# One hybrid block, sixteen-head attention: the first unit's score rows inside the preparation, and row statistics taken tile by tile for the next layer

## The reference, cut to what matters

```python
x = x + A(_layernorm(x))      # gated slot attention
x = x + FFN(_layernorm(x))    # 16-head causal attention, then a mixture of 4 experts, with norms of its own
x = x + C(_layernorm(x))      # 16 heads of 16, not causal
x = x + FFN(_layernorm(x))

def _layernorm(x, axis=-1, eps=1e-05):
    m = jnp.mean(x, axis=axis, keepdims=True)
    v = jnp.var(x, axis=axis, keepdims=True)
    return (x - m) / jnp.sqrt(v + eps)

def C(x, q_w, k_w, v_w, q_b, k_b, v_b, out_w, out_b):   # cut
    q, k = apply_rope(heads(x @ q_w.T + q_b)), apply_rope(heads(x @ k_w.T + k_b))
    attn = jnp.einsum('bhqd,bhkd->bhqk', q, k) * scaling
    out = jnp.einsum('bhqk,bhkd->bhqd', softmax(attn), heads(x @ v_w.T + v_b))
    return merge(out) @ out_w.T + out_b
```

## Time and profile before

| | |
|---|---|
| median of 3 runs | 2630.3 us |
| lowest, highest | 2629.23, 2631.29 us |
| the profiled execution | 2630.27 us |
| its span in the trace | 2628.5 us |
| TensorE busy | 2331.3 us (89%) |
| VectorE, ScalarE, POOL busy | 1678.3, 1192.8, 1100.5 us |
| mean granted TensorE clock | 0.963 |

### The profile page before, as it was taken

The page is one execution under the profiler, slowest core; times in us unless marked ns, Lnnn a source line. Parts: engine busy times, 40 slices in busy tenths (PEclk is TensorE's granted clock), DMA queues, the critical chain, the costliest instruction groups (busy, mean ns, idle before and its releaser), DMA issues. The chain is left out here.

```text
span 2628.5 us, 49074 instructions
## 1 busy us (share of the span) xinstructions
PE 2331.3 (89%) x18400; PEld 1614.6 (61%) x18400; DVE 1678.3 (64%) x3286; ACT 1192.8 (45%) x2937; POOL 1100.5 (42%) x1264
## 2 busy tenths in 40 slices
PE   5888888888888889888858999999889989999999
PEld 3467754777547775477745666677533356666685
DVE  3857777577776777667726777752366557777613
ACT  3655465554554546545424555532115535555411
POOL 0367632676326763277634544430030025444300
PEclk9999999999999999999978999999889989999999
DMA  2100000000010000000004000000100030000000
GB/s 46 49 6 2 2 17 32 6 2 2 17 33 5 3 2 17 17 2 2 2 1 120 19 19 19 7 1 1 49 1 1 1 114 19 19 19 13 1 1 17
DMA packets 57625, 46.30 MB, mean 18 GB/s; under 512 B 11560, under 2 KB 50864, under 8 KB 57008
## 3 DMA queue, kind: packets, MB, share of 16 engines
q1 hardware_dynamic: 57392, 43.16, 5.6%
HBM read 42.10 MB, written 1.05 MB: 16 GB/s over the span
## 5 line engine op out<-in xcount | busy, mean ns | idle before, releaser
L1153 DVE SCALAR_TENSOR_TENSOR work<-four,taps,work 128x511 f32<-128x511 f32 (+2 forms) x384 | 284.7, 748 | 127.1 <-ACT work L849 117.5
L1761 POOL TENSOR_TENSOR rot<-q_plain,ropes 128x512 f32<-128x512 f32 x64 | 81.0, 1266 | 574.7 <-ACT q_plain L1792 574.7
L599 PE MATMUL four<-xT,wring 128*128 128x512 f32 x512 | 252.8, 621 | 6.6 <-DMA wring<-in_Wk_dram 4.8
L906 ACT ACTIVATE work<-four 128x512 f32<-128x512 f32 x216 | 129.0, 597 | 269.4 <-PE four L678 243.4
L729 PE MATMUL four<-work 128*128 128x128 f32 x1536 | 217.0, 286 | 0.0
L1805 ACT ACTIVATE pr<-four,nmaxf 128x512 f32<-128x512 f32 (+3 forms) x256 | 133.8, 525 | 171.4 <-DVE nmaxf L1643 171.4
L1643 DVE TENSOR_REDUCE nmaxf<-four 128x1 f32<-128x512 f32 (+3 forms) x256 | 125.7, 491 | 125.6 <-PE four L1486 120.8
L729 PEld LDWEIGHTS four<-work 128*128 128x128 f32 x1536 | 193.4, 196 | 3.9
L1484 PE MATMUL four<-rot,rot 128*128 128x512 f32 (+3 forms) x512 | 179.5, 446 | 5.5 <-DVE rot L1635 3.8
L1088 POOL TENSOR_TENSOR work<-work 128x256 f32<-128x256 f32 x184 | 145.6, 791 | 78.0 <-DVE work L1217 57.4
L1095 POOL TENSOR_TENSOR work<-work 128x256 f32<-128x256 f32 x184 | 141.7, 770 | 84.2 <-PE bank L763 74.6
(11 more groups left out here) (266 smaller groups left out, 5430.9 us busy)
## 6 DMA issues: line engine op xcount, KB each, us to landing
wqkv<-in_f_wq_dram SPq DMA_DIRECT2D x32, 128.0 KB, 2.3
wqkv<-in_f_wk_dram SPq DMA_DIRECT2D x32, 128.0 KB, 2.4
wqkv<-in_f_wv_dram SPq DMA_DIRECT2D x32, 128.0 KB, 2.4
wo<-in_f_wo_dram SPq DMA_DIRECT2D x2, 2048.0 KB, 11.7
we<-in_f_we_dram SPq DMA_DIRECT2D x4, 1024.0 KB
wring<-in_Wk_dram SPq DMA_DIRECT2D x4, 512.0 KB, 3.8
wring<-in_Ww_dram SPq DMA_DIRECT2D x4, 512.0 KB
wring<-in_Wv_dram SPq DMA_DIRECT2D x4, 512.0 KB, 3.9
```

The source lines that it names most:

```text
L599: last = nc.tensor.matmul(unit_bank(i)[:], wring[n % 2][:, c, h * P:(h + 1) * P], k.xT[:, c, b * T:(b + 1) * T], start=(c == 0), stop=(c = ...
L906: nc.scalar.activation(turned_keys(s, l), b3(key_bank), ACT.Copy).then_inc(key_kept, 1)
L1153: ins = nc.vector.scalar_tensor_tensor(out=cbuf[i % 4][:, n:], in0=unit_bank(i)[:, 0:T - n], scalar=taps[:, {"q": 0, "k": 1}.get(kind, 2), ...
```

## The change

It has two parts.

The first moves the row statistics. A new function `measure` takes the statistics and the aggregate of one tile, each after a wait. A, B (not D) and C call it directly after their last add to a tile, and the next layer's norm only waits for the eight. The first norm of all, before A, is as it was.

The second moves the first unit's four row groups: after the turns of parts 4, 7, 10 and 13 on TensorE, and their maxima after the rotations of parts 5, 8, 11 and 14 on VectorE. Since the groups need the banks 0 to 3, projections go to banks 4 and 5 and turns to 6 and 7. VectorE waits for POOL's zeroed tiles before the first part and not before the values.

```diff
+def measure(k, dve, stage, t):
+    nc, signal = k.nc, k.measured[stage]
+    nc.vector.bn_stats(k.stats[:, t, :], k.x[:, t, :]).then_inc(signal, 1)
+    dve.wait_ge(signal, 2 * t + 1)
+    nc.vector.bn_aggr(k.mean_var[:, t, :], k.stats[:, t, :]).then_inc(signal, 1)
...
-            for t in range(NT):
-                last = nc.vector.bn_stats(k.stats[:, t, :], src[:, t, :])
-            then(last)
-            for t in range(NT):
-                last = nc.vector.bn_aggr(k.mean_var[:, t, :], k.stats[:, t, :])
-            then(last)
+            if measured is None:
...
+            else:
+                dve.wait_ge(k.measured[measured], 2 * NT)
...
                             if t >= 2:
                                 add(g, t - 2)
-                        add(g, NT - 2)
-                        add(g, NT - 1)
+                                dve.wait_ge(x_added, (g - 1) * NT + t)
+                                measure(k, dve, 0, t - 2)
+                        for t in (NT - 2, NT - 1):
+                            add(g, t)
+                            dve.wait_ge(x_added, (g - 1) * NT + t + 2)
+                            measure(k, dve, 0, t)
...
-                for t in range(NT):
-                    last = nc.vector.bn_stats(k.stats[:, t, :], k.x[:, t, :])
-                last.then_inc(x_stats, 1)
-                dve.wait_ge(x_stats, 1)
-                for t in range(NT):
-                    last = nc.vector.bn_aggr(k.mean_var[:, t, :], k.stats[:, t, :])
-                last.then_inc(x_stats, 1)
-                dve.wait_ge(x_stats, 2)
+                dve.wait_ge(k.measured[2 * rep], 2 * NT)
...
+                        if n >= E * NT and rows is None:
+                            dve.wait_ge(y_used, n + 1)
+                            measure(k, dve, 1, t)
...
+FIRST_ROWS = {4 + 3 * r: r for r in range(CH)}
...
-                        last = nc.tensor.matmul(k.bank[i % 2][:], wqk[m][:, c, j * P:(j + 1) * P], k.xT[:, c, b * T:(b + 1) * T],
+                        last = nc.tensor.matmul(part_bank(i)[:], wqk[m][:, c, j * P:(j + 1) * P], k.xT[:, c, b * T:(b + 1) * T],
...
-                    nc.tensor.matmul(k.bank[2 + i % 2][:], turn_m[:], flat[i % 3][:], start=True, stop=True).then_inc(c_turned, 1)
+                    nc.tensor.matmul(part_turn_bank(i)[:], turn_m[:], flat[i % 3][:], start=True, stop=True).then_inc(c_turned, 1)
+                    if i in FIRST_ROWS:
+                        pe.wait_ge(c_roped, 2)
+                        score_rows(0, FIRST_ROWS[i])
...
                     for r in range(CH):
-                        if n < NC_UNITS:
+                        if 0 < n < NC_UNITS:
                             score_rows(n, r)
...
                     nc.vector.tensor_tensor(qk[m][:, j, b * T:(b + 1) * T], cs[n % 2][:], sn[n % 2][:], ALU.add).then_inc(c_roped, 1)
+                    if n - 1 in FIRST_ROWS:
+                        maximum(0, FIRST_ROWS[n - 1])
...
                     nc.vector.tensor_tensor(k.x[:, t], k.x[:, t], k.bank[t % 4][:, 0:D], ALU.add).then_inc(added, 1)
+                    dve.wait_ge(added, t + 1)
+                    measure(k, dve, 2, t)
```

## The result

| | before | after |
|---|---|---|
| median | 2630.98 us (7 runs) | 2619.26 us (7 runs, 2616.99 to 2624.64) |
| ratio | | 0.9960, 95% interval 0.9949 to 0.9970 |
| the profiled execution | 2630.27 us | 2616.99 us |
| its span | 2628.5 us | 2615.2 us |

The changed kernel is faster by 0.4%, 11.7 us by the medians and 13.3 by the two profiled executions; 13.7 was forecast. The profiled execution of after is the fastest of its seven.

A forecast was written before the change was run, and what follows sets the result against it. The attention start was taken as a ping-pong of TensorE and VectorE, the preparation as a TensorE stream with room on VectorE. Terms -1.75 - 1.74 + 2.1 - 12.3 = -13.7 from 2630.27 gave 2616.6 us, range 2612 to 2622.

The forecast's parts named there:

- first seam: Slot attention to expert block: statistics after each add bring the norm's root 1.75 us earlier, and all of it arrives.
- third seam: Attention to expert block: statistics after each add bring the norm's root 1.74 us earlier.
- second seam, tail: Expert block to attention: statistics make VectorE the pace of the last eight scaled adds, ending 2.1 us later.
- second seam, transfers: Attention's first projection awaits the last of ten transfers, which move with the block's start; nothing won back, 0.
- four groups: Four row groups added to TensorE's gapless preparation stream, 0.97 us each, 3.9 us in all.
- fourth maximum: On VectorE between the rotations of parts 14 and 15, on the path for 2.3 us; the first three cost nothing.
- clock falls in the pause: TensorE's pause before the third value tile grows to 3.5 us, the clock falls, 2.0 us lost.
- row stage gone: The first unit's row groups after the values vanish, shift transposes follow the last value tile at once: -17.07 us.
- first unit at the full clock: TensorE reaches the shift from a dense value stream at full level, so the first unit gains 3.4 us.
- rival of a broken stream: Preparation: a row group takes 2.09 us because its 32-row pieces must wait; 2621.1 us in all, chance 0.08.
- holds: Rival: the clock holds over the pause before the third value tile; 2614.6 us in all, chance 0.14.
- two rivals with a low first unit or slow units: Clock low from values into first unit, 2623.5 us, chance 0.09; units at the 1.2 GHz level, 2640 us, 0.03.

The follow-up runs named there:

- e8: Changed kernel with the fourth maximum taken by VectorE after its part of the value tiles; median 2616.18 us, ratio 0.9964 to before.
- e1: Changed kernel with row groups moved but without the statistics at the adds, each norm taking its own; median 2620.44 us, ratio 0.9966 to before.
- e6: Changed kernel with the preparation awaiting six of the ten transfers, the other four awaited at the values; median 2612.28 us, ratio 0.9930 to before.
- e3: Changed kernel without statistics in the expert block, its scaled adds bare, the two other seams keeping theirs; median 2616.20 us, ratio 0.9949 to before.
- e7: Changed kernel with each of the four row groups in the preparation issued twice; 2616.47 us in one run.
- e4: Changed kernel with the row groups one part earlier, behind parts 3, 6, 9 and 12; median 2619.72 us, ratio 0.9962 to before.
- e9: Changed kernel with the row groups two parts earlier, behind parts 2, 5, 8 and 11; median 2613.83 us, ratio 0.9942 to before.
- e2: Changed kernel with statistics kept but the row groups back after the values; median 2629.88 us, ratio 0.9996 to before.
- e5: Changed kernel with the row groups two parts apart, behind parts 3, 5, 7 and 9; median 2619.18 us, ratio 0.9956 to before.
- b1: Changed kernel with the edits of e5, e6 and e3 together; median 2615.22 us, ratio 0.9939 to before.
- b2: Changed kernel with the edits of e5 and e6 together; median 2614.27 us, ratio 0.9938 to before.
- b3: Changed kernel with the edits of e9, e6 and e3 together; median 2609.58 us, ratio 0.9923 to before.

## Why the prediction was right, and where its sizes were off

The mechanism held: the row stage is gone, the groups run inside the preparation without a wait, and both expert seams are shorter. The sum held too: -13.7 forecast, -13.3 between the profiled executions, -11.7 between the medians, whose 2619.26 is 2.7 us over the forecast of 2616.6.

| step | forecast | measured, and in which run |
|---|---|---|
| first seam | -1.75 | -1.76 |
| third seam | -1.74 | -1.75 to the root, -2.10 to the projection |
| second seam, tail | +2.1 | +2.06 |
| second seam, transfers | 0 | +1.13 |
| four groups | +3.9 | +4.85 (P; +5.06 beyond the first turn) |
| fourth maximum | +2.3 | +2.04 (V; e8) |
| clock falls in the pause | +2.0 | +1.69 in after, e1, e6; 0 in e3, e7 |
| row stage gone | -17.07 | -17.07 (S: 23.03 to 5.96 where the clock held) |
| first unit at the full clock | -3.4 | -3.70 |

The rest, -0.2, -0.2 and 0.0, is the time up to the first add, the first expert block up to its last eight scaled adds, and everything from the second shift to the last add of the attention and from the last block's first projection on.

That the sum came within 0.4 us of the difference between the two profiled executions is in part luck. Transfers and groups cost 2.1 us more than forecast; the third seam, the fourth maximum, the clock, the first unit and the rest gave 1.7 more.

1. *Seams one and three.* Right to 0.01 at the root. The table load came to be what the root waits for, as the forecast said, and no transfer took the gain. The 0.35 more at the third seam is in the transposes ahead of the projection (2.58 us from the first one, 2.93 before): the granted clock was still 1.00 from 2110 to 2111 and fell during them, while before it was 0.50 throughout. Ten other executions with these statistics took 7.57 to 7.59 us for the seam, so the change's share is 1.75.
2. *Second seam.* The bound of two prices for a tile, 1.06 to 1.15, was taken at 1.07; it is 1.06. That nothing comes back was right too, and e3 shows it: without these statistics N is the same. The forecast's "move with it" was not exact: N was 15.20 in after. Nine other executions with all ten transfers awaited gave 13.57 to 14.56, with and without the statistics; so most of the 1.13 is the chance of that execution, not a price of the change.
3. *The groups.* The step mis-sized by most: 0.97 each. P grew by 4.85; beyond the first turn it grew by 5.06 (37.96 to 43.02, the same 43.02 in e1, e3, e4, e8 and e9), 1.27 each. The group's own length was read from one that stood alone, where nothing stands close enough to be held up; between full-height products 0.42 comes on top (e7). The stream itself runs at 0.86, so the forecast was too high there and left out what comes on top. The rival of a broken stream (2.09 each) is refuted: no group took more than 1.14.
4. *The fourth maximum.* Right place, 2.04 instead of 2.3: the sine product behind it starts 2.20 after it, and the last sum took 1.03 us instead of 1.19. That the first three cost nothing was right: no TensorE wait stands before them.
5. *The clock.* The forecast let it fall (2.0) and made "holds" a rival at 14%. In after it fell for 1.69. But a pause of the same 3.25 us brought a fall in after, e1 and e6 and none in e3 and e7. So the size of the pause does not decide it: from these five executions, the term would be estimated as 3 in 5 of 1.7, 1.0 us. The forecast's ground was also misread in part. It said that three pauses of 2.4 us had brought the clock down in the row stage of before; by the stretches of that trace it was at 1.00 until 1953.9 and fell within the first of the three (1952.5 to 1954.9). The Trainium skill, "TensorE: Matmul & The Clock Gate", section "Why this matters for your kernels", says that long idle gaps between bursts of matmuls drop the clock. The traces of after, e1 and e6 agree, those of e3 and e7, with the same gap, do not.
6. *The first unit.* Dense values did bring the full level along: U 15.93 in all runs with the rows moved, whether the clock fell in the values or not. The size leans on the profiled execution of before: e2, with the same first unit behind the same row stage, took 17.56 and not 19.63, since its clock came back sooner, and against it the gain is 1.6, not 3.7. The two rivals with a low first unit or slow units are out: the next unit took 16.26 as before.

The difference between -13.3 and -11.7 is open. Single runs of one kernel spread over 8 us and more, and in the profiled executions the stretch from the expert block's first projection to its last eight scaled adds, which no kernel here changes, lay between 487.4 and 494.7 us. No run here tells what sets it.

## What to carry to other kernels

Move a ping-pong of two engines into an earlier stretch where the first is the bound and the second has room, but price it by the difference of a part with and without it, not by the length of the moved instructions; and give the second engine as many parts behind the last one as it needs to catch up (here three of 2.57 us leave 0.33 of a maximum of 2.28), or its last piece stands on the path. Work moved ahead of a barrier pays only if the seam behind it is bound by what the work feeds: the same statistics gained 1.75 us where the norm bounded the next block and lost 2.06 where transfers did. Before shortening a seam, look at which transfers its first instruction awaits that it does not read: to await them later was worth 5 us here.

## What was not expected of the hardware

- The clock falls on the same stretch of instructions in some executions only. Value products behind a pause of 3.25 us: 7.13 us with the fall (after, e1, e6), 5.45 without (e3, e7). Behind 2.57 it fell (e4), behind 2.81 ahead of the shift it held (e8), behind 1.21 to 1.54 it held in before, e2, e5, e8, e9, b1, b2, b3. In b3 it fell in the last unit, where TensorE's pauses were 0.7 us, and so it did in e5 and b2, in b1 somewhat earlier: from the second shift to the last add these four took 131.1 to 131.2 us, the ten others 129.5. No run tells why. Behind the row stage, which e2 and before share, it was back at the full level sooner in e2 (U 17.56 us, 19.63 before).
- With ten transfers issued in one row, the products that await them all start 13.57 to 15.20 us after the block's start (ten executions); the six that are needed first, put at the head, let the products start after 9.2 to 10.2 (four executions).
- A group of products on 32 rows among full-height ones costs 0.42 us once, beyond its own 0.86, though TensorE shows no idle time around it (after, e7).
